# The last of eight group sums moves from VectorE to a pair of identity matmuls, and its load and stores change queues

## The chip, the cores and the metric

One Trainium2 chip, one core. The metric is the device time of one execution in microseconds (us), measured around the whole kernel. The trace of one profiled execution gives a span, from the first to the last instruction of the core, which is a little shorter than the device time.

## The reference

One block of a network for 4 sequences of 1024 tokens with 128 features each. An adaptive layernorm is followed by a small network whose weights are trained on the way (1024 gradient steps in a scan), then a second adaptive layernorm by a mixture of experts: 8 experts of which each token takes 2, and one shared expert. Only the end of it matters here:

```python
acc = jnp.einsum('btf,df->btd', hs, Ws2) + bs2            # shared expert
...
y = jnp.einsum('btef,edf->bted', h, W2) + b2
acc = acc + jnp.einsum('bted,bte->btd', y, gates)         # two experts of each token
return SCALE * acc
...
x = x + gb * _L0_ffn_ref(h, ...)
```

So a token's output is its running value `x`, plus `gb` times (the shared expert's row, plus two gated expert rows).

## The kernel before

The expert stage goes over tiles of 256 token rows, 39 of them, each of one expert (`JOBS` mixes them with tiles of the shared expert). For each expert tile PE does two layers of matmuls, ACT the activation between them, DVE adds the bias and multiplies by the token's gate, and POOL scatters the 256 rows to the DRAM tensor `ys` by two indirect DMAs. In `ys` the two expert rows of a token lie side by side.

The end of the kernel brings these rows back. The 32 chunks of tokens form 8 groups (`NG`) of 4 chunks, a group being a tile of 128 partitions by 4 chunks by 128 features. For each group `g`:

- `load(eng, g)` (L1274) fetches the rows of `ys` into `yg[g]`, 512 KB, 128 x 4 x 256: the first 128 of a row are one expert's result, the last 128 the other's. It raises `s_yg[g]` by 16 when it has landed.
- `group_step(3g)` (L1871) on DVE adds the two halves into `ysum`; `group_step(3g+1)` (L1874) multiplies by `gate[:, 1, :]` (the factor `gb`); `group_step(3g+2)` (L1878) adds the result to `xr`, which already holds the residual and the shared expert, and raises `fin_ready`.
- `store(eng, g)` (L1279) waits for `fin_ready` to reach `g + 1` and writes the group to the output with one DMA of 64 KB for each of the 4 sequences.

The order of the work is written out by hand, one instruction stream for each engine. SP and ACT issue the loads and stores, each through its own hardware DMA queue (q1 is SP's and q10 ACT's); an instruction stream stops at a wait, so whatever stands behind the wait on the same engine waits too. `scattered(eng, n)` waits until the scatters of the first `n` tiles have landed, and stands ahead of the loads that need them. The last two groups need all 39 tiles (`scattered(..., N_TILES)`). SP ends with a wait for all stores (`s_out`).

PE's last work before the change is the second layer of the last shared tile (L1456). Bank 7 of PSUM was used by `fed(j)` for odd tiles `j`; the last tile's number is 38.

Of the kernel before, what the change touches and what calls it, by code (L numbers as in the profile page):

```python
# [6 lines left out]
ALU = mybir.AluOpType  # L7
# [6 lines left out]
P = 128  # L14
B, S, D = 4, 1024, 128
# [4 lines left out]
GRP = 4  # L20
NG = CH // GRP
# [11 lines left out]
N_TILES = (2 * B * S) // TS + E - 1  # L33
# [27 lines left out]
def program(nc, x, w_q, w_kv, w1, b1, w2, b2, w_router,  # L61
            s_w1t, s_b1, s_w2t, s_b2, cond, w_mod, slabs, ident_in, before_in, lower_in, tabs_in, xs, ys, out):
    with ExitStack() as ctx:
        ctx.enter_context(nc.allow_non_contiguous_dma(reason="small transposed operands"))

        def sb(name, shape, dt=F32):
            return ctx.enter_context(nc.sbuf_tensor(name, shape, dt))
# [3 lines left out]
        def sem(name):  # L71
            return ctx.enter_context(nc.semaphore(name))
# [6 lines left out]
        bank = [ctx.enter_context(nc.psum_tensor(f"bank{i}", [P, 512], F32)) for i in range(8)]  # L79
# [3 lines left out]
        xr = sb("xr", [P, CH, D])  # L83
# [6 lines left out]
        gate = sb("gate", [P, 2, D])  # L90
# [11 lines left out]
        ident = sb("ident", [P, P])  # L102
# [44 lines left out]
        with ExitStack() as stack, block() as blk:  # L147
# [13 lines left out]
            @blk.sync  # L161
            def _(sp):
                for q in range(4):
                    cs = slice(q * QUARTER, (q + 1) * QUARTER)
                    for b in range(B):
                        sp.dma_start(xr[b * STEPS:(b + 1) * STEPS, cs, :],
                                     x[b].rearrange("(c t) d -> t c d", t=STEPS)[:, cs, :]).then_inc(s_x[q], 16)
                sp.dma_start(tabs[:, :], tabs_in).then_inc(s_b, 16)
                sp.dma_start(mkh[:, :], lower_in).then_inc(s_b, 16)
                sp.dma_start(wrT[:, :], w_router.rearrange("e d -> d e")).then_inc(s_b, 16)  # L170
                sp.dma_start(sb1[:, :], s_b1.rearrange("(n p) -> p n", p=P)).then_inc(s_b, 16)
                for k in range(SUB):
                    sp.dma_start(bs2row[:, k * D:(k + 1) * D], s_b2.rearrange("(o d) -> o d", o=1)).then_inc(s_b, 16)
                sp.wait_ge(s_b, 16 * 6)
# [1022 lines left out]
        with block() as blk:  # L1197
# [5 lines left out]
            yg = [psb(f"yg{i}", [P, GRP, 2 * D]) for i in range(NG)]  # L1203
# [25 lines left out]
            ysum = [psb(f"ysum{i}", [P, GRP, D]) for i in range(2)]  # L1229
# [19 lines left out]
            s_yg = [sem(f"s_yg{i}") for i in range(NG)]  # L1249
            s_slab = [sem(f"s_slab{i}") for i in range(RW)]  # L1250
            meta_step, meta_ready = sem("meta_step"), sem("meta_ready")
            fin_ready, s_out = sem("fin_ready"), sem("s_out")
            sum_used = sem("sum_used")
            e_tx, e_hg, e_u, e_x, e_y, e_yb, e_yo = (sem(f"e_{n}") for n in "tx hg u x y yb yo".split())
            out_v = [out[b].rearrange("(c t) d -> t c d", t=STEPS) for b in range(B)]
# [13 lines left out]
            def scattered(eng, n):  # L1269
                for r in range(RY):  # L1270
                    eng.wait_ge(s_sc[r], 16 * SUB * len(range(r, n, RY)))

            def load(eng, g):
                eng.dma_start(yg[g][:, :, :], ys_v[:, g * GRP:(g + 1) * GRP, :]).then_inc(s_yg[g], 16)  # L1274

            def store(eng, g, bs=range(B)):
                eng.wait_ge(fin_ready, g + 1)
                for b in bs:
                    eng.dma_start(out_v[b][:, g * GRP:(g + 1) * GRP, :],  # L1279
                                 xr[b * STEPS:(b + 1) * STEPS, g * GRP:(g + 1) * GRP, :]).then_inc(s_out, 16)  # L1280

# [6 lines left out]
            @blk.sync  # L1288
            def _(sp):
                def weights(j):  # L1290
                    if j >= RW:
                        sp.wait_ge(e_yb, job["expert", j - RW] + 1)
                    e = sp.value_load(e_i[0:1, j:j + 1], min_val=0, max_val=E - 1)
                    sp.dma_start(slab[j % RW][:, :], slabs[:, bass.ds(e, 1), :].rearrange("p o w -> p (o w)")).then_inc(s_slab[j % RW], 16)

                def rows(j):
                    if j >= RX:
                        sp.wait_ge(e_tx, j - RX + 1)
                        sp.wait_ge(meta_ready, j - RX + 1)
                    row = sp.value_load(row_i[0:1, j:j + 1], min_val=0, max_val=XS_ROWS - TS)  # L1300
                    sp.dma_start(xt[j % RX][:, :, :], xs[bass.ds(row, TS), :].rearrange("(s p) w -> p s w", p=P)).then_inc(s_xt[j % RX], 16)

                sp.wait_ge(table_ready, 2)
                for j in range(RW):
                    weights(j)
                sp.wait_ge(s_half[0], 16 * CH)
                for j in range(N_FULL):
                    rows(j)
                    if j >= RW:
                        weights(j)  # L1310
                sp.wait_ge(table_ready, 4)
                weights(N_FULL)
                weights(N_FULL + 1)
                sp.wait_ge(s_half[1], 16 * CH)
                for j in range(N_FULL, N_TILES):
                    rows(j)
                    if j >= N_FULL + 2:
                        weights(j)
                    if j == LOAD_AT:
                        scattered(sp, BY_HALF)  # L1320
                    if LOAD_AT <= j < LOAD_AT + 4:
                        load(sp, j - LOAD_AT)
                scattered(sp, BY_THREE)
                load(sp, 4)
                load(sp, 5)
                store(sp, 0)
                store(sp, 2)
                scattered(sp, N_TILES)
                load(sp, 6)
                store(sp, 4)  # L1330
                store(sp, 6)
                store(sp, 7, range(0, B // 2))
                sp.wait_ge(s_out, 16 * B * NG)

            @blk.tensor
            def _(pe):
# [90 lines left out]
                def feed_for(i):  # L1427
                    if i < len(JOBS) and JOBS[i][0] == "expert":
                        feed(JOBS[i][1])
# [16 lines left out]
                def e_down(i):  # L1446
                    kind, j = JOBS[i]
                    y = bank[4 + i % 2]
                    if i >= 2:
                        pe.wait_ge(e_yb, i - 1)  # L1450
                    for s in range(SUB):
                        for n in range(FT):
                            if s == 0:
                                pe.wait_ge(e_x, FT * i + n + 1)
                            right = slab[j % RW][:, F + n * P:F + (n + 1) * P] if kind == "expert" else sw[:, 1, n, :]
                            mm = pe.matmul(y[:, s * D:(s + 1) * D], hid[i % 2][:, n, s * P:(s + 1) * P], right,  # L1456
                                           start=(n == 0), stop=(n == FT - 1), skip_group_check=True)
                    mm.then_inc(e_y, 1)
# [65 lines left out]
                for i in range(len(JOBS)):  # L1524
                    feed_for(i + 2)
                    if i + 1 < len(JOBS):
                        e_up(i + 1)
                    e_down(i)

            @blk.scalar  # L1530
            def _(act):
# [103 lines left out]
                    gelu(t)  # L1635
                for i in range(len(JOBS)):
                    e_gelu(i)
                store(act, 1)
                store(act, 3)
                scattered(act, N_TILES)  # L1640
                load(act, 7)
                store(act, 5)
                store(act, 7, range(B // 2, B))

            @blk.vector
            def _(dve):
# [219 lines left out]
                def group_step(k):  # L1866
                    g = k // 3
                    y, xc = ysum[g % 2][:, :, :], xr[:, g * GRP:(g + 1) * GRP, :]
                    if k % 3 == 0:
                        dve.wait_ge(s_yg[g], 16)  # L1870
                        dve.tensor_tensor(y, yg[g][:, :, 0:D], yg[g][:, :, D:2 * D], ALU.add).then_inc(sum_used, 1)  # L1871
                    elif k % 3 == 1:
                        dve.wait_ge(sum_used, 2 * g + 1)
                        dve.tensor_tensor(y, y, gate[:, 1, :].unsqueeze(1).broadcast_to([P, GRP, D]), ALU.mult).then_inc(sum_used, 1)  # L1874
                    else:
                        dve.wait_ge(sum_used, 2 * g + 2)
                        dve.wait_ge(sh_ready, min(N_SH, (g + 1) * GRP // SUB))
                        dve.tensor_tensor(xc, y, xc, ALU.add).then_inc(fin_ready, 1)  # L1878
# [126 lines left out]
                for k in range(14, 18):  # L2005
                    group_step(k)
                dve.wait_ge(sh_ready, N_SH)
                for k in range(18, 24):
                    group_step(k)

            @blk.gpsimd
            def _(pool):
# [122 lines left out]
```

## Time and profile before

| | |
|---|---|
| median of 3 runs | 631.76 us |
| lowest, highest | 629.91, 633.92 us |
| the profiled execution, device time | 631.76 us |
| its span | 630.0 us |
| mean granted TensorE clock | 0.969 |
| PE, DVE, ACT, POOL busy | 90%, 70%, 53%, 62% of the span |

Device time less span is 1.76 us, which lies around the traced instructions. Busy shares are means over the whole span; in the last 11 us PE does nothing, and DVE is busy for 7.5 us of them.

### The profile page before, as it was taken

The numbers are of one execution on the slowest core, as the hardware profiler recorded it, in microseconds if no ns is written. First come the engines' busy times: TensorE is split into PE (matmuls) and PEld (weight loads), VectorE is DVE, ScalarE is ACT, GpSimd is POOL, SyncE is SP. The second block draws the span as 40 slices with busy tenths as digits, with TensorE's granted clock in tenths as the row PEclk, the third lists the DMA queues.
The fourth block names the chain that finished last, engine by engine and source line by source line (L and its number), as shares of the span: only waits on it lengthen the run. The fifth ranks groups of instructions, "written<-read, shape, count | busy, mean of one in ns | idle before, by whom it ended". The sixth has DMA issues, their size and how long they took to land. (4 is left out here: it accounts for less than half of the span.)

```text
span 630.0 us, 14425 instructions
## 1 busy us (share of the span) xinstructions
PE 565.8 (90%) x4292; PEld 509.7 (81%) x4292; DVE 438.0 (70%) x1744; ACT 332.2 (53%) x1064; POOL 390.9 (62%) x598
## 2 busy tenths in 40 slices
PE   2469999999999999999997778879979999999993
PEld 2349999899998999999985467768869999999992
DVE  3736888888888788888886488984584554444567
ACT  2455666666566666666653265676334434444441
POOL 1525566666656666665662606888888887777661
PEclk9999999999999999999999678799999999999997
DMA  9069930000000000000000000126454767777956
GB/s 202 1 267 394 395 152 1 2 0 0 0 0 0 0 0 0 0 0 0 1 3 1 2 1 31 45 81 229 118 151 133 206 181 224 228 244 245 351 175 179
DMA packets 39796, 66.77 MB, mean 106 GB/s; under 512 B 7522, under 2 KB 26724, under 8 KB 39748
## 3 DMA queue, kind: packets, MB, share of 16 engines
q1 hardware_dynamic: 31220, 54.45, 27.5%
q0 software_dynamic: 4544, 9.45, 4.2%
q10 hardware_dynamic: 3984, 2.30, 1.5%
q8 instruction: 22, 0.36, 0.2%
q14 instruction: 26, 0.21, 0.1%
HBM read 36.26 MB, written 29.92 MB: 105 GB/s over the span
## 5 line engine op out<-in xcount | busy, mean ns | idle before, releaser
L1582 ACT ACTIVATE hid<-bank,slab 128x256 f32<-128x256 f32 x156 | 63.1, 472 | 84.9 <-PE bank L1442 69.8
L2045 POOL DMA_INDIRECT ys<-yo,dst x78 | 75.9, 973 | 36.3 <-DVE yo L1922 18.1
L2037 POOL DMA_INDIRECT xs<-hrow,slot_i x64 | 63.6, 994 | 35.8 <-issue 35.8
L1442 PE MATMUL bank<-hg,slab 128*128 128x256 f32 x312 | 74.0, 381 | 4.5 <-issue 4.1
L1456 PEld LDWEIGHTS bank<-slab,hid 128*128 128x128 f32 x624 | 75.8, 192 | 2.0
L1456 PE MATMUL bank<-slab,hid 128*128 128x128 f32 x624 | 76.0, 275 | 0.0
L1442 PEld LDWEIGHTS bank<-hg,slab 128*128 128x128 f32 x312 | 56.3, 190 | 11.5 <-issue 5.2
L1917 DVE TENSOR_TENSOR yb<-bank,slab 128x256 f32<-128x256 f32 x39 | 16.6, 425 | 64.3 <-PE bank L1456 46.4
L990 POOL TENSOR_TENSOR nL<-aL,ones 128x128 f32<-128x128 bf16 x32 | 16.9, 527 | 42.2 <-ACT aL L699 42.2
L413 PE MATMUL bank<-aH,W2p 128*128 128x128 f32 x192 | 42.4, 303 | 0.1
L413 PE MATMUL bank<-kv,W1b 128*128 128x128 f32 x192 | 41.4, 298 | 0.0
L1002 POOL TENSOR_TENSOR nH<-aH,ones 128x128 f32<-128x128 f32 x32 | 14.6, 455 | 36.7 <-ACT aH L717 36.7
L2020 POOL MEMSET rested<- 128x1408 f32 x25 | 32.2, 1288 | 0.0
L413 PEld LDWEIGHTS bank<-aH,W2p 128*128 128x128 f32 x192 | 29.1, 191 | 3.4 <-DVE W2p L794 0.3
L413 PE MATMUL bank<-GX,ge 128*128 128x128 f32 x128 | 30.7, 322 | 0.6 <-DVE ge L794 0.5
L994 POOL TENSOR_TENSOR oL<-tL,ones 128x128 f32<-128x128 f32 x32 | 14.5, 454 | 24.7 <-ACT tL L702 24.7
L413 PEld LDWEIGHTS bank<-kv,W1b 128*128 128x128 f32 x192 | 29.8, 196 | 0.1
L1922 DVE TENSOR_SCALAR yo<-yb,gt 128x128 f32<-128x128 f32 x78 | 27.1, 446 | 1.4
L1017 POOL TENSOR_TENSOR diff<-ge 128x256 f32<-128x256 f32 x32 | 23.3, 728 | 5.5 <-DVE sums L797 5.5
L794 DVE SCALAR_TENSOR_TENSOR gL<-qrowL,bank 128x128 bf16<-128x128 bf16 x64 | 18.4, 288 | 11.1 <-ACT qrowL L710 5.6
L974 POOL TENSOR_TENSOR GXb<-GX,ones 128x256 bf16<-128x256 f32 x32 | 23.3, 727 | 4.2 <-DVE GX L794 2.1
L413 PE MATMUL bank<-hT,wkv 128*128 (+1 forms) x128 | 23.3, 307 | 2.5 <-POOL arowL L1037 2.5
(349 smaller groups left out, 1873.0 us busy)
## 6 DMA issues: line engine op xcount, KB each, us to landing
slab<-in_slabs_dram SPq DMA_DIRECT2D x39, 578.0 KB
xs<-fill SPq DMA_DIRECT2D x34, 528.0 KB
xt<-xs SPq DMA_DIRECT2D x39, 132.0 KB
yg<-ys SPq DMA_DIRECT2D x7, 512.0 KB, 4.5
xr<-in_L_attn_x_dram SPq DMA_DIRECT2D x16, 128.0 KB, 6.7
ys<-yo,dst POOLq DMA_INDIRECT x78
out_dram<-xr SPq DMA_DIRECT2D x18, 64.0 KB
xs<-hrow,slot_i POOLq DMA_INDIRECT x64
```

What stands on the lines that cost most here:

```text
L413: return pe.matmul(dst, lhs, rhs, start=start, stop=stop, skip_group_check=True)
L794: return dve.scalar_tensor_tensor(out=dst, in0=a, scalar=s, in1=b, op0=o0, op1=o1)
L974: pool.tensor_tensor(GXb[r][:, :, :].rearrange("p k t -> p (k t)"), GX[r][:, :, :].rearrange("p k t -> p (k t)"), ones2[:, :], ALU.mult).t ...
L990: pool.tensor_tensor(nL[1][:, :], aL[1][:, :], ones2[:, 0:P], ALU.subtract).then_inc(l_n, 1)
L1017: pool.tensor_tensor(diff[:, :, :], ge[r % 2][1][:, :, :], ge[r % 2][0][:, :, :], ALU.subtract).then_inc(chk_d, 1)
L1442: mm = pe.matmul(e_half(i, n), left[:, n * P:(n + 1) * P], right, start=True, stop=True)
L1456: mm = pe.matmul(y[:, s * D:(s + 1) * D], hid[i % 2][:, n, s * P:(s + 1) * P], right, start=(n == 0), stop=(n == FT - 1), skip_group_check ...
L1582: nc.scalar.activation(hid[i % 2][:, n, :], e_half(i, n), ACT.Gelu_apprx_tanh, bias=bias).then_inc(e_x, 1)
L1922: dve.tensor_scalar(yo[v][:, s, :], yb[i % 2][:, s, :], gt[v][:, s:s + 1], None, ALU.mult).then_inc(e_yo, 1)
L2020: nc.gpsimd.memset(rested[:, :], 0.0).then_inc(pause_done, 1)
L2037: pool.indirect_dma_start(out=xs[:, :], out_offset=bass.IndirectOffsetOnAxis(ap=slot_i[:, i, c:c + 1], axis=0), in_=hrow[:, c, :], in_offs ...
L2045: pool.indirect_dma_start(out=ys[:, :], out_offset=bass.IndirectOffsetOnAxis(ap=dst[v][:, s:s + 1], axis=0), in_=yo[v][:, s, :], in_offset ...
```

## The change

Only the end of the program is touched, and of the eight groups only the last, group 7.

- PE gets two matmuls at its end, with the identity as stationary operand and the two halves of `yg[7]` as moving ones, accumulated into bank 7: their sum. They wait for the load.
- DVE's addition of the halves (L1871) of group 7 is dropped. Its multiplication by the gate now reads bank 7 and waits for the matmuls; the addition to `xr` follows as before.
- The load of group 7 moves from ACT's queue to SP's, right behind the load of group 6. ACT no longer waits for the scatters.
- The stores of group 7 were two DMAs on each queue; now all four are on ACT's.

```diff
-            def store(eng, g, bs=range(B)):
+            def store(eng, g):
                 eng.wait_ge(fin_ready, g + 1)
-                for b in bs:
+                for b in range(B):
...
                 scattered(sp, N_TILES)
                 load(sp, 6)
+                load(sp, 7)
                 store(sp, 4)
                 store(sp, 6)
-                store(sp, 7, range(0, B // 2))
                 sp.wait_ge(s_out, 16 * B * NG)
...
                     e_down(i)
+                pe.wait_ge(s_yg[NG - 1], 16)
+                for k in range(2):
+                    mm = pe.matmul(bank[7][:, :], ident[:, :], yg[NG - 1][:, :, k * D:(k + 1) * D], start=(k == 0), stop=(k == 1))
+                mm.then_inc(sum_ready, 1)
...
                     e_gelu(i)
-                store(act, 1)
-                store(act, 3)
-                scattered(act, N_TILES)
-                load(act, 7)
-                store(act, 5)
-                store(act, 7, range(B // 2, B))
+                for g in range(1, NG, 2):
+                    store(act, g)
...
-                for k in range(18, 24):
+                for k in range(18, 21):
                     group_step(k)
+                g = NG - 1
+                dve.wait_ge(sum_ready, 1)
+                dve.tensor_tensor(ysum[g % 2][:, :, :], bank[7][:, :].rearrange("p (c d) -> p c d", c=GRP),
+                                  gate[:, 1, :].unsqueeze(1).broadcast_to([P, GRP, D]), ALU.mult).then_inc(sum_used, 1)
+                dve.wait_ge(sum_used, 2 * (NG - 1) + 1)
+                xc = xr[:, g * GRP:(g + 1) * GRP, :]
+                dve.tensor_tensor(xc, ysum[g % 2][:, :, :], xc, ALU.add).then_inc(fin_ready, 1)
```

On DVE, the end of the program: the last group loses one of its three steps, and the first of the two that are left reads a PSUM bank. The names are output tile and inputs.

```order
@@ -1057,6 +1057,5 @@
 L1874 TENSOR_TENSOR ysum<-ysum,gate 128x512
 L1878 TENSOR_TENSOR xr<-ysum,xr 128x512
-L1871 TENSOR_TENSOR ysum<-yg 128x512
-L1874 TENSOR_TENSOR ysum<-ysum,gate 128x512
-L1878 TENSOR_TENSOR xr<-ysum,xr 128x512
+L2012 TENSOR_TENSOR ysum<-bank,gate 128x512
+L2016 TENSOR_TENSOR xr<-ysum,xr 128x512
 L1197 UNCONDITIONAL_BRANCH
```

The dropped step turns up at the end of PE's program, as the two matmuls behind the last shared tile:

```order
@@ -931,3 +931,4 @@
 L1442 MATMUL bank<-hT,sw 128x256 x4
 L1456 MATMUL bank<-sw,hid 128x128 x16
+L1531 MATMUL bank<-yg,ident 128x512 x2
 L1197 UNCONDITIONAL_BRANCH
```

On SP's queue, the last loads (L1274) and stores (L1279); these are the four stores of groups 0 and 2, then the last loads, then the other stores:

```order
@@ -342,5 +342,5 @@
 L1274 DMA yg<-ys 128x1024 x2
 L1279 DMA out_dram<-xr 32x4x128 x8
-L1274 DMA yg<-ys 128x1024
-L1279 DMA out_dram<-xr 32x4x128 x10
+L1274 DMA yg<-ys 128x1024 x2
+L1279 DMA out_dram<-xr 32x4x128 x8
 L1197 UNCONDITIONAL_BRANCH
```

SP has one load more and two stores fewer; ACT has the reverse, and its 16 stores follow one another.

## Rows read from the trace of the kernel before

**Rows 1.** Chain that ended last, 612 to 631 us: start us, us, what.

```profile
612.08 1.82 PE bank L1456 x16
...
619.26 3.56 DMA yg<-ys
```

**Rows 2.** Timeline, DVE in the last 10 us: start us, us, instruction [idle before].

```profile
622.91 0.69 DVE L1871 TENSOR_TENSOR ysum<-yg 128x512 f32<-128x512 f32 x1 [0.17 <-DMA yg<-ys]
...
624.36 0.69 DVE L1878 TENSOR_TENSOR xr<-ysum,xr 128x512 f32<-128x512 f32 x1
624.97 0.68 DVE L1871 TENSOR_TENSOR ysum<-yg 128x512 f32<-128x512 f32 x1
625.69 0.69 DVE L1874 TENSOR_TENSOR ysum<-ysum,gate 128x512 f32<-128x512 f32 x1
626.41 0.69 DVE L1878 TENSOR_TENSOR xr<-ysum,xr 128x512 f32<-128x512 f32 x1
```

**Rows 3.** DMA issues, 619 to 620 us: tiles, count, KB each, us to landing.

```profile
yg<-ys ACTq DMA_DIRECT2D x1, 512.0 KB, 4.3
```

**Rows 4.** Timeline, DMA issues of the tail on both queues.

```profile
619.26 0.34 SPq L1274 DMA_DIRECT2D yg<-ys  x1
619.86 0.36 ACTq L1274 DMA_DIRECT2D yg<-ys  x1
...
625.08 1.77 SPq L1279 DMA_DIRECT2D out_dram<-xr  x4
...
627.13 0.79 SPq L1279 DMA_DIRECT2D out_dram<-xr  x2
```

**Rows 5.** DMA queues, 620 to 622, then 622 to 624 us: packets, MB, share.

```profile
q1 hardware_dynamic: 120, 0.47, 81.1%
...
q10 hardware_dynamic: 141, 0.51, 66.5%
q1 hardware_dynamic: 360, 0.21, 33.5%
```

**Rows 6.** Timeline, PE, 350 to 371 us.

```profile
352.04 3.62 PE L1340 MATMUL bank<-hT,wz 128*128 128x512 f32 x4
...
363.01 1.95 PE L1348 MATMUL bank<-W2p,yg 128*128 128x128 f32 x16
367.83 0.66 PE L1357 MATMUL bank<-ident,xn 128*128 128x128 f32 x4 [2.87 <-ACT xn L1543]
```

**Rows 7.** Timeline, ACT, 352 to 364 us: the readers of the matmuls L1340.

```profile
355.69 0.69 ACT L1534 ACTIVATE yg<-bank,W1b 128x512 f32<-128x512 f32 x1 [1.02 <-PE bank L1340]
358.54 0.69 ACT L1534 ACTIVATE yg<-bank,W1b 128x512 f32<-128x512 f32 x1 [2.16 <-PE bank L1340]
359.40 0.69 ACT L1534 ACTIVATE yg<-bank,W1b 128x512 f32<-128x512 f32 x1 [0.17 <-PE bank L1340]
```

**Rows 8.** PE by windows: window us, PE busy (instructions), granted clock, DMA share, GB/s.

```profile
352.00:353.00 1.00, 1.00 (x4) 0.50 0.00 0
358.00:360.00 2.00, 2.00 (x6) 1.00 0.00 0
369.00:370.00 1.00, 0.64 (x4) 0.81 0.00 0
619.00:620.00 1.00, 0.16 (x2) 1.00 0.55 133
622.00:623.00 1.00, 0.00 (x0) 0.60 0.99 373
```

**Rows 9.** Instructions of L1340 and L1651: ns min/median/max, first and last start.

```profile
L1340 PEld LDWEIGHTS bank<-hT,wz x3: 333/333/337, 351.8 to 352.9; 128*128 128x128 f32 x3
...
L1651 DVE SCALAR_TENSOR_TENSOR yg<-bank,gate x8: 673/682/692, 356.8 to 391.6; 128x512 f32<-128x512 f32 x8
```

**Rows 10.** DMA queues, 625 to 628, then 628 to 630 us.

```profile
q1 hardware_dynamic: 589, 0.27, 38.0%
...
q10 hardware_dynamic: 288, 0.13, 22.5%
```

More of the change, by code:

```diff
@@ L1251, in program @@
             meta_step, meta_ready = sem("meta_step"), sem("meta_ready")
-            fin_ready, s_out = sem("fin_ready"), sem("s_out")
+            sum_ready, fin_ready, s_out = sem("sum_ready"), sem("fin_ready"), sem("s_out")
             sum_used = sem("sum_used")
```

## The prediction

> **What bounds the kernel now.** I began with the chain of waits [rows 1]. The reader is to see that PE's expert matmuls at 612.08 us stand on it, and behind them, by way of the last scatter, the load of group 6 (issued 619.26, 3.56 us long) with DVE's steps after it. From there to the end PE isn't on the chain. So whatever the change does, it does in the last 11 us, and the 612 us before can move only by chance: the order of the instructions there is the same in both programs.
>
> Within these 11 us three things matter. The timeline of DVE [rows 2] shows six steps that follow each other every 0.7 us, with an idle gap of 0.17 us only before the first, which ends with a DMA. So from 622.91 to 627.10 (626.41 plus 0.69) DVE itself is the bound. The DMA issues [rows 3, 4] show when the input of group 7 is there: its load was issued at 619.86 and took 4.3 us, so it landed near 624.2, some 0.8 us before DVE came to it at 624.97. And the windows [rows 8] show that PE, which did its last matmul in the window at 619, lost its clock in the window at 622: a mean of 0.60 between 1.0 and 0.5 puts the fall 0.2 us into it, at 622.2.
>
> **The step removed.** One DVE addition, 0.68 us, with its handshake 0.72 (624.97 to 625.69). That is all that can be gained: group 6 holds DVE until 625.05 (624.36 plus 0.69) in either program, so group 7 can't be taken up earlier than now, only be shorter by this step.
>
> **The load.** Now it stands on SP's queue behind the load of group 6. Its issue moves from 619.86 to some 619.6 (619.26 plus 0.34). But issue isn't its limit. In 620 to 622 us q1 moved 0.47 MB, and in 622 to 624 q10 moved 0.51 MB [rows 5]: the two loads (512 KB each) already passed one after the other, and the window at 622 shows 373 GB/s at a DMA share of 0.99 [rows 8], so nothing is left for them to share better. By data alone the second lands 512 KB / 373 GB/s = 1.4 us behind the first: 622.82 + 1.4 = 624.2, the same as now. In 622 to 624 q1 also moved 0.21 MB of stores, which in one queue come behind the load rather than beside it; that could give 0.5 us at most. I take 624.2, with 623.7 as the early bound. The late one is the load's own full 3.56 us after the landing of the first, 626.4, if one queue did not overlap two loads.
>
> **The two matmuls.** The trace has the same shape: each L1340 matmul is 128x128 by 128x512 in f32 and leaves two records, so the four records from 352.04 [rows 6] are two matmuls, as many as are added here. They were at the granted clock 0.50 [rows 8], the level of 1.2 GHz, and the reader of the second started at 355.69 [rows 7]: 3.65 us from the start of the first matmul to its consumer. At clock 1.00, 2.4 GHz, two of them took some 1.9 us (the readers at 358.54 and 359.40 are 0.86 apart, so 2 x 0.86 plus 0.2 until the reader starts).
>
> Which of the two? The matmuls start near 624.5, 5.3 us after PE's last work at 619.16. The clock fell here 3.0 us after that work ended. Elsewhere it fell 4.7 us after the end of dense work, in spite of a burst of 0.66 us between (work ends 364.96 [rows 6]; the 0.81 at 369 means 369.6 [rows 8]). Neither pause kept the clock for 5.3 us. I take the half clock, 3.65 us, and keep 1.9 as the bound.
>
> The Trainium skill, "TensorE: Matmul & The Clock Gate", section "Why this matters for your kernels", says to leave no gaps of more than some 3 us between bursts of matmuls, or the clock goes back to half. The trace agrees: 3.0 us of pause sufficed here, and by that rule the sum keeps its 3.65; without it this term would be 1.9 and the time 1.75 us less.
>
> Ahead of the first matmul stand the wake-up and the load of the identity. A weight load at half clock lasts 0.33 us [rows 9] and the matmul starts before it is over (351.8 against 352.04). I take 0.3 us, between 0.2 and 0.5. First matmul 624.5, result usable 628.15.
>
> **DVE behind them.** Two steps. The multiplication reads PSUM; a DVE step of this size that reads a bank lasts 0.68 us at the median, between 0.67 and 0.69 [rows 9], as long as the one that reads SBUF. 0.72 + 0.69 = 1.41 us: the last addition ends at 629.55, where now it ends at 627.10. **This part costs 2.45 us.** DVE's own queue holds nothing else behind the new wait, and PE's nothing but its end; the only ones that wait are the two DVE steps and the stores of group 7.
>
> **The stores.** Two DMAs on each of two queues become four on one. Four issues in a row took 1.77 us, two took 0.79 [rows 4], so the last one is issued 0.98 later. What it does to the data: store 6 is the pattern of four on one queue. Its first issue is at 625.08, and q1 moved 589 packets from 625 to 628 us; two DMAs make 288 packets (what q10 moved for its half of store 7 [rows 10]), four make 576, so it was over at about 628.0, 2.9 us after its first issue. Store 7 on two queues was issued from 627.13, and the span ended at 630.0, 2.9 us later including the last receipt and SP's final wait, some 0.85 us. 2.9 + 0.85 - 2.9 = 0.85; bounds 0.5 and 1.0, and I take **0.8 us**. ACT does its other stores as before, and without the load and its wait it can't be late for this one.
>
> The skill's page "DMA: Bandwidth & Descriptors", section "Issuing engines are not separate DMA queues", has it that issuing from several engines saves only the time of issue, as all run on the same DMA engines. By that the loss would be the 0.98 of the issues and the load's move would cost nothing; the rows give 0.8 and nothing, so the two differ by 0.2 us. No row here yet shows store 7 alone on one queue.
>
> **The sum.** 630.0 + 2.45 + 0.8 = 633.25 us of span, and with the 1.76 us around it 635.0 us. The profiled execution's time equals the median of the three runs, so nothing is to be corrected. It is 0.5% slower. About 1%, 6.3 us, is what a measurement of this kernel can tell from no change (its own three runs spread over 4.0 us), so I expect "no change that can be told", from the slow side.
>
> **Rivals.**
> (1) *The clock holds.* The fall takes up to 4.7 us of pause in these rows, and the matmuls come after 5.3; were the early landing and the late fall to meet, the term is 1.9 instead of 3.65, and the time 633.3. For it: the one slow fall. Against it: both had fallen by then.
> (2) *The step is gained.* If the pair were done before DVE is free at 625.05, DVE would lose one step, -0.72, and if the stores cost nothing either, the time is 631.0. That needs a landing before 623.0 with the clock at full, and rows 5 leave no DMA time for this. With the store's 0.8 even this case is at 631.8, no gain.
> (3) *One queue holds the second load back.* If the load of group 7 only starts when that of group 6 has landed, it lands at 626.4, 2.2 us later than in my sum, and all of it is on the path: 637.2, slower by 0.9%. It decides against the forecast of no visible change from a landing at about 627.3 on. Against it: q1 has carried back-to-back loads at the full DMA share for most of 620 to 622, one load only.
> (4) *The change doesn't do what it says*, i.e. the pair is off the path because the load lands far later for other reasons or DVE is late: I see no mechanism, as DVE has nothing else left.
>
> **How the numbers follow.** Forecast 0.75, (1) 0.12, (2) 0.03, (3) 0.08, (4) and the unexpected 0.02. The forecast's own bounds: load -0.5, lead -0.1 or +0.2, stores -0.3 or +0.2, together 634.1 to 635.4. To these comes what a median of some runs moves by chance, about 1.5 us to each side by the spread of 629.91 to 633.92. With (1) at 633.3 inside and (3) at the upper end, the range is 631.5 to 637.5. Faster by over 1% (below 625.4) has no case, 0.02 for chance; slower by over 1% (above 638.1) needs (3) and some more on top, 0.08; within 1% holds 0.90.
>
> **What would show it.** In the new profile PE has four records of 128x512 at the very end, about 1.0 us each, with a granted clock of 0.50 there; two if the records are joined. DVE idles from 625.05 until about 628.1, released by PE and not by a DMA; two DVE steps follow. The landing of the last load is within 0.5 us of 624.2 if the tail starts at the same time. The four last issues are on ACT's queue, over 1.8 us, and the span ends 3.6 to 3.9 us after the last DVE step. The chain of waits goes through PE again for its last 4 us. It would be wrong if the clock in the last stretch reads 1.00, if the load lands more than 1 us later than its neighbour's 1.4 allows, or if the matmuls of this shape from an operand that was just written by DMA were slower than L1340's.

## The result, and the profile after

The changed kernel took 636.52 us (median of 10 runs, 635.18 to 639.68) against 632.01 us (10 runs, 629.91 to 633.92): ratio 1.0082, 95% interval 1.0059 to 1.0104. That is slower by less than 1%. The ratio on record is worked out from the single runs and is not the quotient of the two medians, which is 1.0071. Runs over 1.5% above the fastest of the same kernel are left out of every ratio, which in one later lot took out ten of the 29 runs of the kernel before, so ratios are the rougher for it. Two later comparisons of the same two kernels, told below, gave 1.0058 and 1.0017.

The profiled execution took 635.87 us, with a span of 634.1. Its chain of waits (start us, us, what) from the last scatter to the end:

```profile
617.58 2.42 DMA ys<-yo,dst
...
620.53 4.73 DMA yg<-ys
625.26 0.04 issue
625.31 3.80 PE bank L1531 x4
629.11 0.03 issue
629.13 0.70 DVE ysum L2012
629.83 0.02 issue
629.86 0.69 DVE xr L2016
```

Where before a load ended on DVE and six DVE steps followed [rows 1, 2], the chain now goes through the load of group 7, the pair of matmuls, and two DVE steps. The timeline of the same stretch shows DVE waiting:

```profile
616.78 3.29 PE L1456 MATMUL bank<-sw,hid 128*128 128x128 f32 x28
...
620.14 0.82 SPq L1274 DMA_DIRECT2D yg<-ys  x2
...
624.03 0.69 DVE L1871 TENSOR_TENSOR ysum<-yg 128x512 f32<-128x512 f32 x1 [0.37 <-DMA yg<-ys]
...
625.31 3.78 PE L1531 MATMUL bank<-yg,ident 128*128 128x512 f32 x4 [5.23 <-DMA yg<-ys]
625.48 0.69 DVE L1878 TENSOR_TENSOR xr<-ysum,xr 128x512 f32<-128x512 f32 x1
...
629.13 0.69 DVE L2012 TENSOR_TENSOR ysum<-bank,gate 128x512 f32<-128x512 f32 x1 [2.96 <-PE bank L1531]
629.86 0.69 DVE L2016 TENSOR_TENSOR xr<-ysum,xr 128x512 f32<-128x512 f32 x1
```

The windows (from and to in us, length; then what PE, weight loads, DVE, ACT and POOL were busy; then granted clock, DMA share, GB/s) show at which clock the pair ran:

```profile
622.00:623.00 1.00, 0.00 (x0) 0.00 (x0) 0.93 (x3) 0.00 (x0) 0.00 (x0) 0.86 1.04 377
...
626.00:627.00 1.00, 1.00 (x2) 0.34 (x1) 0.17 (x1) 0.00 (x0) 0.00 (x0) 0.50 0.30 82
...
629.00:630.00 1.00, 0.09 (x1) 0.00 (x0) 0.84 (x2) 0.00 (x0) 0.00 (x0) 0.72 0.00 0
```

PE's last matmul of the layers ended at 620.07 (616.78 + 3.29), its clock fell in the window at 622 (0.86 puts it at 622.7, 2.7 us later), was 0.50 while the pair ran, and rose in the window at 629, as the pair was just over. The four stores of the last group in the timeline of ACT's queue:

```profile
630.58 1.79 ACTq L1279 DMA_DIRECT2D out_dram<-xr  x4
```

and ACT's two in a kernel that still has them on two queues (`sum_only`, below):

```profile
630.30 0.86 ACTq L1279 DMA_DIRECT2D out_dram<-xr  x2
```

Everything ahead of the tail moves from one execution to the next: the load of group 6 was issued at 619.26 in the trace before and at 620.14 here, and later traces of this very kernel have it at 625.84 and 619.76. So the fair measure of the change is the **tail**, from the issue of the load of group 6 to the end of the span. It was 10.74 us (630.0 - 619.26) and is 13.96 (634.1 - 620.14), with unrounded spans: 3.2 us longer.

### The profile page after: what moved, and what is told of

It is laid out like the page before. It is cut to its first block and busy times, and to the rows that moved or that the text cites. A ratio compares the mean times of both kernels' runs of the same rounds, so it can differ in the third digit from the quotient of the medians.

```text
span 634.1 us, 14426 instructions
## 1 busy us (share of the span) xinstructions
PE 570.1 (90%) x4296; PEld 512.1 (81%) x4296; DVE 443.8 (70%) x1743; ACT 333.6 (53%) x1064; POOL 391.1 (62%) x598
## 5 line engine op out<-in xcount | busy, mean ns | idle before, releaser
L1922 DVE TENSOR_SCALAR yo<-yb,gt 128x128 f32<-128x128 f32 x78 | 34.3, 613 | 1.4
```

The source lines that it names most:

```text
L1922: dve.tensor_scalar(yo[v][:, s, :], yb[i % 2][:, s, :], gt[v][:, s:s + 1], None, ALU.mult).then_inc(e_yo, 1)
```

## The experiments

For each run the tail is split at the end of DVE's last step: from the load's issue to it, and from it to the end of the span. After the first comparison the kernels ran in three more lots, each with the kernel before beside it. Tail and its parts are in us, each from one trace.

| kernel | ratio to before (95%) | tail | to DVE's end | DVE's end to the end |
|---|---|---|---|---|
| before | | 10.74 | 7.84 | 2.90 |
| changed | 1.0082 (1.0059 to 1.0104) | 13.96 | 10.41 | 3.55 |
| sum_only | 1.0047 (1.0016 to 1.0077) | 12.96 | 10.13 | 2.83 |
| queues_only | 1.0016 (0.9981 to 1.0051) | 11.25 | 7.68 | 3.57 |
| again | 1.0058 (1.0024 to 1.0092) | 13.76 | 10.18 | 3.58 |
| warm5 | 1.0010 (0.9976 to 1.0044) | 13.70 | 10.13 | 3.57 |
| warm6 | 1.0049 (1.0007 to 1.0091) | 11.88 | 8.32 | 3.56 |
| warm8 | 1.0028 (0.9982 to 1.0074) | 13.49 | 9.93 | 3.56 |
| spare_sem | 0.9998 (0.9958 to 1.0039) | 10.82 | 7.98 | 2.84 |
| pool_share | 1.0114 (1.0046 to 1.0181) | 17.35 | 7.78 | 9.57 |
| warm6_split | 0.9996 (0.9953 to 1.0038) | 12.28 | 9.48 | 2.80 |
| stores_split | 1.0026 (0.9983 to 1.0069) | 13.00 | 10.14 | 2.86 |
| pool_late | 1.0021 (0.9979 to 1.0062) | 14.47 | 7.93 | 6.54 |
| again2 | 1.0017 (0.9980 to 1.0055) | 14.44 | 10.88 | 3.56 |

The ratios of the later lots are uncertain by 0.3 to 0.7% (the kernel before spread from 623.24 to 634.38 us in one of them), so most differences between experiments are read from the tails. In the last lot (`warm6_split`, `stores_split`, `pool_late`, `again2`) the kernel before has 18 runs from 625.2 to 628.8 us, 17 from 631.6 to 634.1, and none between. So a ratio there depends on how many of a kernel's runs fall on which side; what decides that the record doesn't show.

**Undoing one half of the change.** `sum_only` takes the pair of matmuls and leaves the queues as before; against the changed kernel:

```diff
                 scattered(sp, N_TILES)
                 load(sp, 6)
-                load(sp, 7)
...
+                store(sp, 7, range(0, B // 2))
...
+                scattered(act, N_TILES)
+                load(act, 7)
+                store(act, 5)
+                store(act, 7, range(B // 2, B))
```

> The sum of group 7 on PE alone; its load stays on ACT's queue, its stores stay two and two. If the time is lost by the pair of matmuls at half clock (my theory), the tail from the issue of the load of group 6 to the end of the span is 13.1 to 13.3 us (10.7 before, 13.9 in the changed kernel), and the whole is 2.4 us above the kernel before. If the queues are what costs (rival: the load behind another load, four stores on one queue), it is 10.7 to 11.3 us and the whole within 0.6 us of before.

`queues_only` takes the queues and leaves all three steps of group 7 on DVE; its edit against the kernel before:

```diff
                 load(sp, 6)
+                load(sp, 7)
...
-                store(sp, 7, range(0, B // 2))
...
+                for g in range(1, NG, 2):
+                    store(act, g)
```

> DVE does all three steps of group 7 as before; its load is on SP's queue behind that of group 6, all four of its stores on ACT's. My theory: the load costs nothing, the stores 0.7 us, so the tail is 11.4 us and the whole is 0.7 us above the kernel before. Rival: one queue holds the second load back, which shows as a landing more than 5.5 us after its issue and an idle gap of DVE before group 7's addition, and 2 us or more on the whole.

The tails are 12.96 and 11.25 us. The matmuls cost 2.2 us, all of it ahead of DVE's end; the queues cost 0.5, of it 0.7 behind DVE's end and nothing (-0.2) ahead of it. Together 2.7 of the 3.2. Most of the rest is how long the loads took in the one trace of each: the pair began 5.17 us after the issue of the first load in the changed kernel and 4.89 in `sum_only`. In the chain of `sum_only` the pair is as long as in the changed kernel, with the load on ACT's queue:

```profile
620.75 4.24 DMA yg<-ys
...
625.03 3.79 PE bank L1531 x4
628.83 0.02 issue
628.85 0.70 DVE ysum L2016
```

In `queues_only` the second load on SP's queue held nothing up: DVE's steps of groups 6 and 7 follow each other without a wait for a load from 624.23 to 628.43 (start us, us):

```profile
624.23 0.69 DVE L1867 TENSOR_TENSOR ysum<-yg 128x512 f32<-128x512 f32 x1
...
626.29 0.69 DVE L1867 TENSOR_TENSOR ysum<-yg 128x512 f32<-128x512 f32 x1
...
627.74 0.69 DVE L1874 TENSOR_TENSOR xr<-ysum,xr 128x512 f32<-128x512 f32 x1
```

The rival of a queue that holds the second load back until the first has landed is out.

**The changed kernel again.**

> The changed kernel as it is, once more beside the others. By the sum of the terms the whole is 3.2 us above before (ratio 1.005). If something ahead of the tail got slower too (rival: the tail began 0.9 us later in its trace), it is 4.5 us above (1.007) again, and the load of group 6 is issued later than in the trace of sum_only, which has the same stream on PE.

1.0058, which is 3.7 us of 636.56, and a tail of 13.76. Its load of group 6 was issued at 625.84, 5.7 us later than in the trace of `sum_only`, which has the same stream of matmuls, and 6.1 later than in `again2`, which is the same kernel. So this stretch moves by some 6 us between executions of one kernel, whatever the change.

**The clock.** `warm5`, `warm6` and `warm8` put more matmuls ahead of PE's wait, of the shape of the pair, from tiles that lie there anyway, into a bank that nobody reads any more (five here, six and eight in the others):

```diff
+                for _ in range(5):
+                    pe.matmul(bank[6][:, :], ident[:, :], sw[:, 1, :, :].rearrange("p n f -> p (n f)"), start=True, stop=True)
                 pe.wait_ge(s_yg[NG - 1], 16)
```

> The changed kernel with five more matmuls of 128x512 on PE between the last shared tile and the wait for the load, from the identity and a weight tile into bank 6, whose result nobody reads. If the half clock is what makes the pair cost 3.8 us (my theory), it keeps the granted clock at 1.00, the reader starts 1.9 to 2.1 us after the first matmul in place of 3.8, and the whole is 1.8 us under the changed kernel, still about 1.4 us above the kernel before. If the duration is bound otherwise (rival: by the operand, fresh from a DMA, or by the strided rows), the clock is 1.00 and the pair still lasts over 3 us.

Five weren't enough. In its timeline the last of them ends at 629.95 and the pair starts at 632.26, after a pause of 2.3 us, and takes nearly as long as before, 3.65 us from its start to its reader at 635.91 against 3.82:

```profile
625.49 4.46 PE L1530 MATMUL bank<-sw,ident 128*128 128x512 f32 x10
632.26 3.62 PE L1533 MATMUL bank<-yg,ident 128*128 128x512 f32 x4 [2.31 <-DMA yg<-ys]
```

and its windows (from and to, length; PE busy, granted clock, DMA share, GB/s) show the clock lost just as the pair begins (0.73 in the window at 632 means that it fell at 632.5):

```profile
631.00:632.00 1.00, 0.00 (x0) 1.00 0.96 326
632.00:633.00 1.00, 0.74 (x1) 0.73 1.13 330
633.00:634.00 1.00, 1.00 (x3) 0.50 0.29 80
```

So it told nothing yet between the clock and the operand, as at clock 1.00 hardly any of the pair ran.

> The changed kernel with six more matmuls of 128x512 on PE ahead of its wait, where the run with five paused 2.3 us and lost the clock 0.2 us after the pair began. PE's last real matmul and the landing of the last load lay 5.0 to 5.3 us apart in most traces, and six matmuls last 5.2 to 5.3 us. If the half clock is what makes the pair cost 3.8 us (my theory), the clock stays at 1.00 through the pair and the reader starts 1.9 to 2.1 us after its first matmul; the tail from the issue of the two loads to the end of the span is 12.2 us in place of 13.8. If the operand or its layout sets the duration (rival), the clock is 1.00 and the pair still lasts over 3 us.

> Eight more matmuls in place of six: they last 6.9 us, so PE doesn't pause at all, but begins the pair some 1.5 us after the landing. My theory: granted clock 1.00 for sure, pair to reader 1.9 to 2.1 us, tail 13.7 us, as long as in the changed kernel: what the clock gives back the late start takes. Rival (the operand sets the duration): pair over 3 us, tail over 15 us.

`warm6` gave the answer. Its timeline of PE:

```profile
619.78 5.32 PE L1530 MATMUL bank<-sw,ident 128*128 128x512 f32 x12
624.93 1.96 PE L1533 MATMUL bank<-yg,ident 128*128 128x512 f32 x4
```

and its windows (columns as for `warm5`):

```profile
624.00:625.00 1.00, 1.00 (x4) 1.00 1.06 333
625.00:626.00 1.00, 1.00 (x4) 1.00 0.87 231
```

The same pair from the same operand takes 1.96 us at clock 1.00 and 3.78 at 0.50. DVE started at 626.93, 2.0 us after the first matmul, and the tail is 11.88 us, 2.1 less than the 13.96 of the changed kernel's first trace (0.3 of it because the pair could begin 4.91 us after the issue of the loads rather than 5.17). Its DVE still ended 0.5 us later than in the kernel before, 8.32 against 7.84: the sum on PE takes 2.0 us from the landing, where DVE's addition is over 0.8 + 0.7 us after it. `warm8` kept the clock too (pair 1.88 us, from 627.71), but its own matmuls ran 7.03 us from 620.84 and pushed the pair back: 13.49 us, about what was expected (13.7). The rival (the operand) is out. The ratios don't tell these kernels apart. `warm6`'s, 1.0049, doesn't show the gain; its interval holds what its tail says (1.1 us over the kernel before, or 1.002). `warm5`'s, 1.0010, shows a gain that its trace doesn't have: by the tail it is 3.0 us behind, or 1.0047, and its interval ends just under that, at 1.0044.

**The stores alone.** `stores_split` is the changed kernel with its last stores two and two again (`store(sp, 7, range(0, B // 2))` at SP's end, `range(B // 2, B)` on ACT).

> The changed kernel with the stores of group 7 two and two on both queues; the load stays on SP's queue, the pair at half clock. Terms add: tail 13.9 - 0.7 = 13.2 us, as long as in the kernel with the sum alone (13.0 us), which had the load on ACT's queue. If the load's queue matters (rival), the two differ by 0.5 us or more.

13.00 us, against 13.2 expected and 12.96 in `sum_only`: between these two traces the load's queue makes no difference. Over all traces that isn't settled. With the load on ACT's queue (five traces) it landed 4.8 to 5.0 us after the issue of group 6's load; with it on SP's, the pair of matmuls began 4.91, 4.91, 4.94, 5.06, 5.17, 5.64 and 6.04 us after it. So it was often as early and sometimes up to 1.1 us later, and no run shows whether the queue or chance makes the late ones. Over all traces the time from DVE's last step to the end is 3.55 to 3.58 us in the seven traces with four stores on one queue and 2.80 to 2.90 in the five with two and two and no late work on POOL: a term of 0.7 us.

**The best of both.**

> The changed kernel with six more matmuls of 128x512 on PE ahead of its wait, and the stores of group 7 two and two on both queues again: the best that the sum on PE can do. If the terms add (my theory), the tail from the issue of the load of group 6 to the end of the span is 11.9 - 0.7 = 11.2 us, still 0.4 us over the 10.7 to 10.9 us of the kernel before, since the pair takes 2.0 us after a landing and DVE would have begun 0.8 us after it: ratio 1.001. Rival: the lost stores were a matter of issue alone and the tail stays at 11.7 us or more.

12.28 us, not 11.2. The stores gave what was expected (2.80 to the end); the loads didn't. Its trace has the pair only at 626.46, 6.04 us after the issue of the loads at 620.42, where `warm6` has 4.91 (624.93 less 620.02); its PE paused 0.95 us, kept the clock, and did the pair in 1.99 us. Why these loads took longer the trace doesn't show, and it is the trace of the longest of its twelve runs (634.55 us), the only trace of this kernel. So whether the two gains add is not shown. Its ratio, 0.9996, is no difference. By the terms (11.88 less 0.7, an estimate) the sum on PE ends at best 0.4 us behind the kernel before, too little for any ratio here to tell. No version that beats the kernel before was found.

**Does the change slow the rest?** `spare_sem` is the kernel before with the semaphore `sum_ready` allocated and unused.

> The kernel before with the new semaphore allocated and not used, which shifts the numbers of some others and nothing else. It tells whether the 0.1 to 0.2% by which the measured ratio exceeds the sum of the tail's terms comes from something the change does to the whole program. Theory (chance): ratio 1.000 within its interval of some 0.003. Rival: 1.002 or more.

0.9998, tail 10.82: none is seen. The interval ends at 1.0039, so it doesn't by itself exclude the 1.002 that was named as the rival.

> The changed kernel once more. The ratio was 1.0082 and then 1.0058, both with intervals of 0.002 to 0.003 to each side; the tail's terms give 3.2 us or 1.005. If the excess is chance in the stretches ahead of the tail, this one falls between 1.002 and 1.008 and the tail is 13.7 to 13.9 us once more.

1.0017, just under the 1.002 expected; its tail was 14.44 us and not 13.7 to 13.9, since its pair started 5.64 us after the issue of the loads (625.40 less 619.76) and not 5.17. Within the two groups of runs of this lot the difference is clearer than in the ratio: by the means `again2` lies 2.7 us above the kernel before in the lower one (8 runs, 627.8 to 630.9 us) and 2.1 us in the upper one (4 runs, 633.5 to 636.0). The three ratios average 1.0052; the tail's 3.2 us are 1.0051. But the intervals of the first (from 1.0059) and of this one (to 1.0055) don't meet, so lots differ by more than their intervals say. The excess of the first comparison is most likely chance; no run shows another cause.

**Trying to beat the kernel before.** If DVE is its bound from the landing of group 6 on, another engine should help. `pool_share` gives POOL one of four chunks of groups 6 and 7, by fewer chunks in DVE's `group_step` and three steps of POOL's own behind its last scatter:

```diff
+                    n = GRP - (g >= NG - 2)
+                    y, xc = ysum[g % 2][:, 0:n, :], xr[:, g * GRP:g * GRP + n, :]
...
+                for g in (NG - 2, NG - 1):
+                    y, c = ysum[g % 2][:, GRP - 1, :], g * GRP + GRP - 1
...
+                    pool.tensor_tensor(y, yg[g][:, GRP - 1, 0:D], yg[g][:, GRP - 1, D:2 * D], ALU.add).then_inc(pool_sum, 1)
+                    pool.wait_ge(pool_sum, 3 * (g - NG + 2) + 1)
+                    pool.tensor_tensor(y, y, gate[:, 1, :], ALU.mult).then_inc(pool_sum, 1)
+                    pool.wait_ge(pool_sum, 3 * (g - NG + 2) + 2)
+                    pool.tensor_tensor(xr[:, c, :], y, xr[:, c, :], ALU.add).then_inc(pool_sum, 1)
```

> The kernel before, with one of the four chunks of groups 6 and 7 taken by POOL for all three steps (128x128 each), and three chunks left to DVE (128x384). If DVE is the bound of the kernel before from the landing of group 6 on (my reading of it), its steps shrink from 0.69 to about 0.56 us, the last ends 0.8 us earlier, and the tail from the issue of group 6's load is 9.9 to 10.1 us against 10.7; on the whole -0.1%, under what the rounds can show. Rival: POOL and DVE get in each other's way, DVE's steps stay at 0.69 or POOL's last step ends after DVE's, and the tail is 10.7 us or more.

Slower, by 1.1% (6.6 us of tail). DVE's share hardly shrank, which is why nothing was gained, and the end of the core came late, which is why it lost. Of its timeline, the steps of both engines for group 6:

```profile
618.54 0.56 DVE L1874 TENSOR_TENSOR ysum<-yg 128x384 f32<-128x384 f32 x1
618.59 0.82 POOL L2102 TENSOR_TENSOR ysum<-yg 128x128 f32<-128x128 f32 x1 [5.29 <-DMA yg<-ys]
619.13 0.69 DVE L1877 TENSOR_TENSOR ysum<-ysum,gate 128x384 f32<-128x384 f32 x1
619.49 0.65 POOL L2104 TENSOR_TENSOR ysum<-ysum,gate 128x128 f32<-128x128 f32 x1
619.86 0.69 DVE L1881 TENSOR_TENSOR xr<-ysum,xr 128x384 f32<-128x384 f32 x1
620.21 0.65 POOL L2106 TENSOR_TENSOR xr<-ysum,xr 128x128 f32<-128x128 f32 x1
620.48 0.80 DVE L1874 TENSOR_TENSOR ysum<-yg 128x384 f32<-128x384 f32 x1
```

Only the first DVE step shrank, to 0.56 us; it began 0.05 us before POOL's first. Of the five that began while POOL worked, four took 0.69 us, like those of 512 elements in the kernel before, and the addition of group 7 at 620.48 took 0.80, where the same addition of group 6 had taken 0.56. That the two engines hinder each other is the likely reading; no run has DVE's steps of 384 elements without POOL. The late end was a surprise: DVE ended at 622.73, POOL at 623.04, the last output packets ran shortly after 625, and the core only at 632.3. `pool_late` asked whether POOL's last instruction sets that end, with one small memset at POOL's end:

```diff
+                pool.wait_ge(s_yg[NG - 1], 16)
+                pool.wait_ge(pause_done, 25)
+                nc.gpsimd.memset(rested[:, 0:P], 0.0)
```

> The kernel before with one small memset on POOL (128x128, a tile that nobody reads) that waits for the load of group 7. It asks why the run in which POOL took a chunk ended 7 us after its last output packet. If the core's end comes a fixed time after POOL's last instruction (theory: 9.3 us there, hidden in the other kernels because POOL ends at 617.7), the span ends about 9.3 us after the memset, 33.5 to 34 us behind 600 if the load lands at 624.2, and the whole is 3 us or more above before. If that wait had another cause (rival), the tail is 10.7 to 10.9 us.

The memset ended at 619.40 and the span at 628.7, 9.3 us later, as POOL's last instruction in `pool_share` (623.04) and the end there (632.3) are 9.3 us apart. The ratio, 1.0021, can't tell 3.7 us more of tail from nothing; the trace can. The memset in its timeline:

```profile
619.20 0.20 POOL L2095 MEMSET rested<- 128x128 f32 x1 [6.62 <-DMA yg<-ys]
```

and SP's last wait in its list of waits (engine and line waited for, us in total, times, longest):

```profile
SPq L1197 <- PEq L1197: 3.8, 1, 3.8
```

That wait is 0.2 us in the kernel before and 6.6 in `pool_share`. The engine named there, PE, had long been done. What POOL does in these 9.3 us the profile doesn't show.

## Why the prediction was right

It said 635.0 us (range 631.5 to 637.5, slower within 1%); measured were 636.52, and 3.2 us more of tail where the sum had 3.25. The mechanism is shown: the half clock by `warm6`, the stores by `queues_only` and `stores_split`. That the tail agrees to 0.03 us is luck: up to DVE's end it grew by 2.57 us (10.41 - 7.84) where the sum had 2.45, behind it by 0.65 (3.55 - 2.90) where it had 0.8. On the whole kernel the medians differ by 4.5 us, 1.3 more than forecast, for which no cause was found.

- **The step removed can give at most 0.72 us.** Nothing of it was gained: DVE ended its group 6 in time (625.48 + 0.69 = 626.17) and then idled 2.96 us.
- **The load's queue costs nothing.** Near enough here, not settled in general. Its landing was put 1.4 us behind the first; here the last issue to landing was 4.73 us and the pair began 5.17 us after the issue of the first load, against 4.9 for the landing before [rows 3, 4]. Between traces this stretch moved from 4.9 to 6.0 us. The prediction's bounds had 0.5 us for an earlier landing and, short of rival (3), nothing for a later one, which was too narrow.
- **The pair runs at half clock, 3.65 us to its reader.** Shown: 3.82 here (625.31 to 629.13), 2.00 in `warm6`. Its reason, a pause of 5.3 us on PE, was shown by `warm6`, which differs only in filling it. The rival "the clock holds", 12%, had little for it: in the traces of the tail the clock fell 2.0 to 3.5 us after PE's last work, and the pause is 5.2. The one slow fall that spoke for it was misread. The 4.7 us before it were no pause: PE worked from 367.83 to 368.49 and again from 369.36, 0.93 us, and the fall at 369.6 lies within that second burst:

```profile
367.83 0.66 PE L1357 MATMUL bank<-ident,xn 128*128 128x128 f32 x4 [2.87 <-ACT xn L1543]
369.36 0.93 PE L1357 MATMUL bank<-ident,xn 128*128 128x128 f32 x4 [0.88 <-ACT xn L1543]
```

- **0.3 us for wake-up and weight load.** Too much: the first matmul started 0.05 us behind the landing (625.26 to 625.31). With 3.82 for 3.65 the two errors nearly cancel (3.87 us from landing to reader, 3.95 in the sum).
- **Two DVE steps, 1.41 us.** 1.42 (629.13 to 630.55); reading PSUM costs nothing extra, 0.69.
- **Stores 0.8 us.** 0.65 in the first pair of traces, 0.7 over all, and by the table it is the steadiest term. It is less than the issue alone (1.79 against 0.86 us, 0.9), as the prediction had from the rows.
- **No effect ahead of the tail.** Supported by `spare_sem` and the three ratios' mean; by their intervals a few tenths of a per cent can't be excluded.

## What to carry over

A step that is moved to an idle engine is priced at that engine's state at that moment. PE, idle for 5 us, works at half its clock, and a sum that costs DVE 0.72 us costs it 3.8; and even at full clock, 2.0. Before taking a step off the bounding engine, look at how long its input is there before the engine comes to it (here 0.8 us): that, plus the step, is all the replacement may take. And the last stores of this kernel were faster on two queues than on one, by 0.7 us, since nothing hides them there.

## What the runs showed of the hardware

- POOL's last instruction stands 9.3 us ahead of the end of the core in the two kernels in which it came late. In the kernel before, POOL ends at 617.65, 12.3 us ahead of the end, and such a stretch would be hidden. So work given to POOL in the last 9 us of this kernel should lengthen it; shown are these two cases.
- With POOL at work beside it, a 128x384 addition on DVE took 0.80 us that had taken 0.56 when it began 0.05 us before POOL's step (`pool_share`). That POOL is the cause is likely, not shown by a run without it.
- How long TensorE keeps its clock after its last matmul varied from trace to trace of the same tail: 2.0 us in `again` (work ended 625.72, the mean of 0.87 in the window at 627 means 627.7), 3.5 in `sum_only` (620.03, and 0.76 in the window at 623). In `warm5` the clock outlived a pause of 2.3 us by 0.2 us only.
